# Starting the FFN products of two tiles one projection group later, with the additions of their banks

## The chip, the cores and the metric

One Trainium2 chip, one core of it. The metric is the device time of one launch in microseconds (us), the median of the runs of one kernel. Engines are named as the profile names them: PE is TensorE (matmuls and transposes), DVE is VectorE, ACT is ScalarE, POOL is GpSimd, SP is SyncE, which issues the DMAs.

## The reference

Input `x` is (8, 1024, 512) in f32. Two branches work on the layer-normed input and are added to it:

```python
xn = layernorm(x)                                   # eps 1e-5
# attention branch
xm = xn * time_mix + shift_by_one_token(xn) * (1 - time_mix)
k = exp(min(xm @ Wk.T, 60)); v = xm @ Wv.T; r = xm @ Wr.T
wkv, sum_k = decayed causal sums over tokens of k*v and of k, per channel
attn = (sigmoid(r) * wkv / (sum_k + 1e-16)) @ Wo.T
# FFN branch: layernorm again (eps 1e-3, gamma, beta), a scale from the
# largest absolute value of the whole tensor, clip to +-128, ternary weight
ffn = clip(xn2 * 128 / gamma) @ w_ternary * (gamma * beta / 128)
out = x + attn + ffn
```

The scale `gamma` of the FFN is a maximum over all eight batches, so no FFN product can start before every batch has been seen. This splits the kernel in two halves.

## The kernel before, in words

A tile is 512 tokens of one batch; a batch has two tiles, 0 and 1. The first half (phase "A") does the attention of batches 0 to 3, writes x + attn of them to a scratch tensor, and prepares the FFN input of all eight batches, with its largest absolute value. The second half (phase "B") does the attention of batches 4 to 7, and the FFN products of all eight: one pass b = 4, 5, 6, 7 handles the tiles of batch b ("own0", "own1") and those of batch b - 4 ("other0", "other1"). The other tiles are read back from scratch into the tile `ZB` ("parked") and the FFN product is added there; the own tiles are added into `X[0]` and `X[1]`.

Each engine has its own program, written out in a fixed order, and semaphores join them. A pass consists of 24 groups, g = 0 to 23. Group g projects one of k, v, r (m = g mod 3) for a chunk c = g div 3 of 128 channels: chunks 0 to 3 are tile 0, chunks 4 to 7 tile 1. A group is 12 matmuls of 512 columns into one bank of `KVR`. Beside it each group works on one of 24 slots: slots 0 to 3 are the four chunks of the FFN input of own0, 4 to 7 of other0, 8 to 11 the time mix of tile 1, 12 to 15 FFN own1, 16 to 19 FFN other1, and 20 to 23 the time mix of the next batch's tile 0. In the second half only the mix slots are transposed on PE. An FFN slot is scaled by ACT (L585), clipped by DVE (L836), split into a high part by ACT (L616, `ffn_hi`) and a low part by DVE (L850, `ffn_lo`). DVE and ACT split slot n while they are at group n + 1: DVE's low part of slot 19, for example, stands at group 20, behind the recurrence of chunk 6 (at group 19), `rwkv_lo` of chunk 5, and the mix of slot 20.

On PE an FFN product (`ffn_out`) is 4 chunks x 4 banks x 2 matmuls = 32 matmuls into the four banks of `OUT`; chunk ch needs the low part of its slot (`dve_lo`). Its place is given by the table `FFN_AFTER`. The attention's output product (`attn_out`) is 4 x 4 x 3 = 48 matmuls into the same four banks: tile 0 behind group 12, tile 1 behind group 23. Its chunk 3 needs DVE's `rwkv_lo` of the last chunk, and in its chunk 0 bank q may only be written when DVE has added the previous contents of bank q to its tile (L942, L944, which count `dve_out`):

```python
if j == 0:
    pe.wait_ge(dve_out, first_bank + q + 1)
```

Where DVE makes these additions is given by the table `ADDS_AT`: group, tile, banks. Within a group of the second half DVE's order is: in groups with m = 2, `rwkv_lo` of the chunk before; the mix or clip of this group's slot (for mix slots it comes first); in the last group of a pass that isn't the last pass, `denominator` of chunk 7, which waits for ACT's logarithm of the sums of chunk 7; the low part of the slot before; the additions of `ADDS_AT`; then, for m = 0, `clamp_k` and `denominator`, for m = 1, `rwkv` of the chunk before and the recurrence of this chunk (L893 to L910). The recurrence of chunk 7 stands at group 22, that of chunk 3 at group 12, behind the additions of that group. The last pass has no slots 20 to 23.

On ACT the evacuation of a mix slot (L575, L576) frees the single transpose bank `TB`, and PE transposes slot n only when slot n - 1 has been evacuated. ACT's evacuation of slot n waits for the low part of slot n - 2.

Of the kernel before, what the change touches and what calls it, by code (L numbers as in the profile page):

```python
# [45 lines left out]

STATS_ORDER = ["other0", "own1", "other1", "next0"]

FFN_AFTER = {4: "own0", 8: "other0", 16: "own1", 20: "other1"}
FFN_TILES = ["own0", "other0", "own1", "other1"]  # L50


# [7 lines left out]
def mixed_decay_kernel(nc, x, time_decay, time_first, time_mix, Wk, Wv, Wr, Wo, Wf, ln_gamma, ln_beta, out):  # L60
# [19 lines left out]
    with ExitStack() as ctx:  # L80
# [330 lines left out]
        def _(pe):  # L411
# [4 lines left out]
            def transpose_slot(b, ph, n, src):  # L416

                _, ch = slot_of(ph, n)
                bank = first_banks[n] if ph == "P" else TB[:, :]
                for q in range(Q):  # L420
                    last = nc.tensor.transpose(bank[:, q * P:(q + 1) * P], src[:, q, ch * P:(ch + 1) * P],  # L421
                                               ident[:, :])
                last.then_inc(pe_t, 1)
# [46 lines left out]
            def project(b, ph, g):  # L470

                c, m = divmod(g, 3)
                t, j = divmod(c, CH)
                w = names[m]
                if m:
                    pe.wait_ge(dve_w, (m + 1) * CH)

                pe.wait_ge((act_k, dve_kv, act_r)[m], CREDIT + CHUNKS * b + c)
                for ch in range(CH):
                    if j == 0 and m == 0:  # L480

                        slot0 = first_slot("mix_own1") if t == 1 else -CH
                        pe.wait_ge(dve_lo, RING + slots_before(b, ph, slot0 + ch) + 1)
                    hi = WH[w][:, ch, j * P:(j + 1) * P]
                    lo = WL[w][:, ch, j * P:(j + 1) * P]
                    nc.tensor.matmul(KVR[:, m, :], hi, XH[t][:, ch, :], start=(ch == 0), stop=False)  # L486
                    nc.tensor.matmul(KVR[:, m, :], hi, XL[t][:, ch, :], start=False, stop=False)  # L487
                    last = nc.tensor.matmul(KVR[:, m, :], lo, XH[t][:, ch, :], start=False, stop=(ch == CH - 1))  # L488
                last.then_inc(pe_g, 1)
# [20 lines left out]
            def ffn_out(b, what):  # L510

                first_bank = bank_use(b, "B", what)
                start_slot = first_slot(f"ffn_{what}")
                for ch in range(CH):
                    pe.wait_ge(dve_lo, RING + slots_before(b, "any", start_slot + ch) + 1)
                    for q in range(Q):
                        if ch == 0:
                            pe.wait_ge(dve_out, first_bank + q + 1)
                        nc.tensor.matmul(OUT[:, q, :], AH[:, ch, q * P:(q + 1) * P], WQ[:, ch, :],  # L519
                                         start=(ch == 0), stop=False)  # L520
                        last = nc.tensor.matmul(OUT[:, q, :], AL[:, ch, q * P:(q + 1) * P], WQ[:, ch, :],  # L521
                                                start=False, stop=(ch == CH - 1))
                        if ch == CH - 1:
                            last.then_inc(pe_out, 1)
                    if ch < CH - 1:
                        last.then_inc(pe_ah, 1)

            def batch(b, ph, is_last=False):
                for g in range(GROUPS):
# [6 lines left out]
                    else:  # L536
                        if n is not None:
                            slot(b, ph, n)
                        project(b, ph, g)
                    if ph == "B" and g in FFN_AFTER:  # L540
                        ffn_out(b, FFN_AFTER[g])
                    if g == ATTN0_AFTER:
# [216 lines left out]
        def _(dve):  # L759
# [166 lines left out]
            def add_out(b, ph, what, banks=None):  # L926
# [12 lines left out]
                for q in range(Q) if banks is None else banks:  # L939
# [3 lines left out]
                    else:  # L943
# [4 lines left out]
            STATS_AT = {4: "own1", 16: "next0"}  # L948

            ADDS_AT = {5: [("own0", [0])], 6: [("own0", [1])], 7: [("own0", [2, 3])],  # L950
# [3 lines left out]

            def batch(b, ph, is_last=False, last_a=False):
                last = None
# [208 lines left out]
```

## Time and profile before

| | |
|---|---|
| median of 3 runs | 951.38 us (951.17 to 952.89) |
| the profiled execution | 954.09 us, span on the core 952.3 us |
| PE busy | 903.3 us, 95% of the span |
| DVE busy | 781.4 us, 82% |
| ACT busy | 522.0 us, 55% |
| POOL busy | 191.0 us, 20% |
| mean granted PE clock | 0.989 of full |

How to read it: a busy PE is not a PE at its peak, since matmuls overlap (each is recorded with some 0.39 us, and the next starts some 0.23 us after it). The second half begins about 465 us from the span's start; passes 5, 6 and 7 begin at about 577, 702 and 827 us. Times below are us from the span's start.

### The profile page before, as it was taken

The numbers are of one execution on the slowest core, as the hardware profiler recorded it, in microseconds if no ns is written. First come the engines' busy times: TensorE is split into PE (matmuls) and PEld (weight loads), VectorE is DVE, ScalarE is ACT, GpSimd is POOL, SyncE is SP. The second block draws the span as 40 slices with busy tenths as digits, with TensorE's granted clock in tenths as the row PEclk, the third lists the DMA queues.
The fourth block names the chain that finished last, engine by engine and source line by source line (L and its number), as shares of the span: only waits on it lengthen the run. The fifth ranks groups of instructions, "written<-read, shape, count | busy, mean of one in ns | idle before, by whom it ended". The sixth has DMA issues, their size and how long they took to land.

```text
span 952.3 us, 13343 instructions
## 1 busy us (share of the span) xinstructions
PE 903.3 (95%) x4162; PEld 734.3 (77%) x4162; DVE 781.4 (82%) x1353; ACT 522.0 (55%) x852; POOL 191.0 (20%) x268
## 2 busy tenths in 40 slices
PE   5689999999999999999999999999999999999998
PEld 5468878777877778777878877778778787787886
DVE  5878898989798989888868887788779787787785
ACT  4366665747574756575554654454646445556442
POOL 4341514234243333240000200202002011020000
PEclk9879999999999999999999999999999999999999
DMA  8120504141422314041504315124052150240502
GB/s 321 66 100 13 200 11 166 66 143 66 143 77 103 118 62 159 28 162 42 189 23 155 111 45 188 32 99 143 27 191 69 58 185 22 98 157 12 175 3 88
DMA packets 50758, 97.89 MB, mean 103 GB/s; under 512 B 3100, under 2 KB 3112, under 8 KB 50728
## 3 DMA queue, kind: packets, MB, share of 16 engines
q1 hardware_dynamic: 50728, 97.54, 29.5%
q8 instruction: 13, 0.21, 0.1%
q14 instruction: 17, 0.14, 0.0%
HBM read 55.58 MB, written 41.94 MB: 102 GB/s over the span
## 4 chain that ended last, share of the span: by engine, by line
DVE 38%; PE 27%; issue 14%; ACT 13%; DMA 3%; POOL 2%; DVEq 1%; ACTq 0%; SPq 0%; POOLq 0%
DVE scans L903 9%; PE kvr L486 5%; PE kvr L488 5%; PE kvr L487 5%; DVE bn_stats L778 4%; DVE rwkv_lo L923 4%; DVE k_and_kv L893 3%; DVE k_and_kv L919 3%; PE out_banks L501 2%; DVE evacuated L826 2%; PE transposed L421 2%; PE out_banks L503 2%; PE out_banks L502 2%; DVE k_and_kv L910 2%; DVE xm_lo L850 2%
## 5 line engine op out<-in xcount | busy, mean ns | idle before, releaser
L1059 POOL TENSOR_SCALAR stat_work<-mean_var 128x4 f32<-128x4 f32 x24 | 7.8, 324 | 549.7 <-DVE mean_var L783 500.7
L519 PE MATMUL out_banks<-w_ternary,ffn_hi 128*128 128x512 f32 x256 | 100.7, 393 | 11.0 <-DVE ffn_lo L850 11.0
L501 PE MATMUL out_banks<-wo_hi,rwkv_hi 128*128 128x512 f32 x256 | 102.6, 401 | 2.0 <-DVE rwkv_lo L923 1.7
L486 PE MATMUL kvr<-xm_hi,wv_hi 128*128 128x512 f32 x256 | 104.5, 408 | 0.0
L486 PE MATMUL kvr<-xm_hi,wk_hi 128*128 128x512 f32 x256 | 104.4, 408 | 0.0
L486 PE MATMUL kvr<-xm_hi,wr_hi 128*128 128x512 f32 x256 | 104.2, 407 | 0.0
L503 PE MATMUL out_banks<-wo_hi,rwkv_lo 128*128 128x512 f32 x256 | 101.3, 396 | 0.0
L502 PE MATMUL out_banks<-wo_lo,rwkv_hi 128*128 128x512 f32 x256 | 101.2, 395 | 0.0
L488 PE MATMUL kvr<-xm_hi,wv_lo 128*128 128x512 f32 x256 | 100.9, 394 | 0.0
L488 PE MATMUL kvr<-xm_hi,wk_lo 128*128 128x512 f32 x256 | 100.9, 394 | 0.0
L487 PE MATMUL kvr<-xm_lo,wv_hi 128*128 128x512 f32 x256 | 100.6, 393 | 0.0
L487 PE MATMUL kvr<-xm_lo,wk_hi 128*128 128x512 f32 x256 | 100.4, 392 | 0.0
L488 PE MATMUL kvr<-xm_hi,wr_lo 128*128 128x512 f32 x256 | 100.4, 392 | 0.0
L521 PE MATMUL out_banks<-w_ternary,ffn_lo 128*128 128x512 f32 x256 | 100.1, 391 | 0.0
L487 PE MATMUL kvr<-xm_lo,wr_hi 128*128 128x512 f32 x256 | 99.7, 389 | 0.0
L1079 POOL TENSOR_SCALAR normed<-x,own_stats 128x512 f32<-128x512 f32 x52 | 78.9, 1524 | 67.6 <-PE transposed L421 59.7
L910 DVE SCALAR_TENSOR_TENSOR k_and_kv<-k_and_kv,first,scans 128x1024 f32<-128x1024 f32 x64 | 84.7, 1324 | 1.1
L580 ACT ACTIVATE evacuated<-transposed,beta_in,gamma_in 128x512 f32<-128x512 f32 x64 | 49.3, 770 | 58.6 <-PE transposed L421 58.6
L903 DVE TENSOR_TENSOR_SCAN scans<-decay,state,k_and_kv 128x512 f32<-128x512 f32 x64 | 79.7, 1289 | 0.0
L903 DVE TENSOR_TENSOR_SCAN scans<-decay,k_and_kv 128x512 f32<-128x512 f32 x64 | 75.0, 1214 | 0.0
L575 ACT ACTIVATE evacuated<-transposed,time_mix 128x512 f32<-128x512 f32 x61 | 41.6, 681 | 58.1 <-PE transposed L421 50.4
L670 ACT ACTIVATE gate<-kvr 128x512 f32<-128x512 f32 x64 | 37.8, 590 | 61.3 <-PE kvr L488 60.9
(125 smaller groups left out, 1988.1 us busy)
## 6 DMA issues: line engine op xcount, KB each, us to landing
x<-in_L_attn_x SPq DMA_DIRECT2D x16, 1024.0 KB, 5.6
ffn_input<-evacuated SPq DMA_DIRECT2D x64, 256.0 KB, 2.4
other<-ffn_input SPq DMA_DIRECT2D x64, 256.0 KB, 2.8
other<-in_L_attn_x SPq DMA_DIRECT2D x8, 1024.0 KB, 5.3
attn_scratch<-x SPq DMA_DIRECT2D x8, 1024.0 KB, 4.4
parked<-attn_scratch SPq DMA_DIRECT2D x8, 1024.0 KB, 6.6
out<-parked SPq DMA_DIRECT2D x8, 1024.0 KB, 4.6
out<-x SPq DMA_DIRECT2D x7, 1024.0 KB, 4.8
```

Source lines behind the costliest of these rows:

```text
L486: nc.tensor.matmul(KVR[:, m, :], hi, XH[t][:, ch, :], start=(ch == 0), stop=False)
L487: nc.tensor.matmul(KVR[:, m, :], hi, XL[t][:, ch, :], start=False, stop=False)
L488: last = nc.tensor.matmul(KVR[:, m, :], lo, XH[t][:, ch, :], start=False, stop=(ch == CH - 1))
L501: nc.tensor.matmul(OUT[:, q, :], hi, WH["o"][:, j, :], start=(j == 0), stop=False)
L502: nc.tensor.matmul(OUT[:, q, :], hi, WL["o"][:, j, :], start=False, stop=False)
L503: last = nc.tensor.matmul(OUT[:, q, :], lo, WH["o"][:, j, :], start=False, stop=(j == CH - 1))
L519: nc.tensor.matmul(OUT[:, q, :], AH[:, ch, q * P:(q + 1) * P], WQ[:, ch, :], start=(ch == 0), stop=False)
L521: last = nc.tensor.matmul(OUT[:, q, :], AL[:, ch, q * P:(q + 1) * P], WQ[:, ch, :], start=False, stop=(ch == CH - 1))
L580: nc.scalar.activation(U[:, r, :], bank, ACT.Identity, bias=bet[:, ch:ch + 1], scale=gam[:, ch:ch + 1]).then_inc(act_u, 1)
L903: last = V.tensor_tensor_scan(S[:, i, 1:TILE + 1], dec, kv[:, i, :], 0.0 if t == 0 else state[:, j, i:i + 1], ALU.mult, ALU.add)
L910: V.scalar_tensor_tensor(kv, kv, first[:, j:j + 1], S[:, :, 0:TILE], ALU.mult, ALU.add).then_inc(dve_sum, 1)
L1079: last = G.tensor_scalar(dst[:, q, :], src[:, q, :], stats[:, 2 * ffn, q:q + 1], stats[:, 2 * ffn + 1, q:q + 1], ALU.mult, ALU.add)
```

## The change

In the second half the FFN products of other0 and other1 are issued by PE behind group 9 and 21 instead of behind group 8 and 20, so they fall behind the transposes of slots 9 and 21 and the k projection of chunks 3 and 7. DVE's additions of other0's banks move from groups 9, 10, 11, 12 (one bank each) to 10 (one), 11 (two) and 12 (one); those of other1 from groups 21 and 22 to 22 and 23, two banks each. Nothing is added or taken out, and the first half is unchanged.

```diff
-FFN_AFTER = {4: "own0", 8: "other0", 16: "own1", 20: "other1"}
+FFN_AFTER = {4: "own0", 9: "other0", 16: "own1", 21: "other1"}
...
             ADDS_AT = {5: [("own0", [0])], 6: [("own0", [1])], 7: [("own0", [2, 3])],
-                       9: [("other0", [0])], 10: [("other0", [1])], 11: [("other0", [2])], 12: [("other0", [3])],
+                       10: [("other0", [0])], 11: [("other0", [1, 2])], 12: [("other0", [3])],
                        17: [("own1", [0])], 18: [("own1", [1])], 19: [("own1", [2, 3])],
-                       21: [("other1", [0, 1])], 22: [("other1", [2, 3])]}
+                       22: [("other1", [0, 1])], 23: [("other1", [2, 3])]}
```

## Rows read from the trace of the kernel before

**Rows 1.** PE's waits from 400 to 952 us: total, times, longest.
```profile
PE out_banks L519 <- DVE ffn_lo L850: 11.0, 7, 2.1
```

**Rows 2.** PE's timeline, other0 of pass 5: start, duration, operation, [idle before <- releaser].
```profile
609.47 0.39 PE L519 MATMUL out_banks<-w_ternary,ffn_hi 128*128 128x512 f32 x1
...
616.16 0.50 PE L519 MATMUL out_banks<-w_ternary,ffn_hi 128*128 128x512 f32 x1 [1.09 <-DVE ffn_lo L850]
...
621.33 0.60 PE L421 MATMUL transposed<-ident,normed 128*128 128x128 f32 x4
...
641.99 0.39 PE L486 MATMUL kvr<-xm_hi,wv_hi 128*128 128x512 f32 x1
```

**Rows 3.** DVE's timeline, the same stretch.
```profile
615.42 0.69 DVE L850 TENSOR_TENSOR ffn_lo<-evacuated,ffn_hi 128x512 fp32r<-128x512 f32 x1
...
630.42 0.68 DVE L893 TENSOR_TENSOR k_and_kv<-k_and_kv,kvr 128x512 f32<-128x512 f32 x1
```

**Rows 4.** PE's timeline, other1 and the output product of pass 5.
```profile
671.49 0.39 PE L519 MATMUL out_banks<-w_ternary,ffn_hi 128*128 128x512 f32 x1
...
678.74 0.50 PE L519 MATMUL out_banks<-w_ternary,ffn_hi 128*128 128x512 f32 x1 [1.65 <-DVE ffn_lo L850]
...
680.69 0.60 PE L421 MATMUL transposed<-ident,normed 128*128 128x128 f32 x4
...
683.90 0.60 PE L421 MATMUL transposed<-ident,normed 128*128 128x128 f32 x4
...
690.30 0.39 PE L501 MATMUL out_banks<-wo_hi,rwkv_hi 128*128 128x512 f32 x1
...
702.15 0.39 PE L486 MATMUL kvr<-xm_hi,wk_hi 128*128 128x512 f32 x1
```

**Rows 5.** ACT's timeline, evacuations of slots 20, 21 and 22 of pass 5.
```profile
671.16 0.68 ACT L576 ACTIVATE shifted_part<-transposed,one_minus_mix 128x512 f32<-128x512 f32 x1
...
681.40 0.69 ACT L575 ACTIVATE evacuated<-transposed,time_mix 128x512 f32<-128x512 f32 x1 [6.95 <-PE transposed L421]
...
685.21 0.68 ACT L575 ACTIVATE evacuated<-transposed,time_mix 128x512 f32<-128x512 f32 x1
```

**Rows 6.** DVE's timeline, groups 20 to 23 of pass 5.
```profile
678.00 0.68 DVE L850 TENSOR_TENSOR ffn_lo<-evacuated,ffn_hi 128x512 fp32r<-128x512 f32 x1
...
686.49 0.15 DVE L823 COPY last_token<-shifted_part 128x1 f32<-128x1 f32 x1 [0.18 <-ACT shifted_part L576]
...
687.76 1.40 DVE L944 SCALAR_TENSOR_TENSOR parked<-out_banks,scalars,parked 128x512 f32<-128x512 f32 x2
...
692.84 1.28 DVE L910 SCALAR_TENSOR_TENSOR k_and_kv<-k_and_kv,first,scans 128x1024 f32<-128x1024 f32 x1
...
695.30 0.69 DVE L915 TENSOR_TENSOR gate<-gate,k_and_kv 128x512 f32<-128x512 f32 x1
695.90 1.29 DVE L850 TENSOR_TENSOR xm_lo<-evacuated,xm_hi 128x512 fp32r<-128x512 f32 x2
```

**Rows 7.** Timeline of the last pass, recurrence and output product of its end.
```profile
936.17 0.69 DVE L893 TENSOR_TENSOR k_and_kv<-k_and_kv,kvr 128x512 f32<-128x512 f32 x1
...
937.65 0.39 PE L501 MATMUL out_banks<-wo_hi,rwkv_hi 128*128 128x512 f32 x1
...
940.53 0.69 DVE L923 TENSOR_TENSOR rwkv_lo<-k_and_kv,rwkv_hi 128x512 fp32r<-128x512 f32 x1
```

**Rows 8.** Stretches: length, busy PE, PEld, DVE, ACT, POOL, PE clock, DMA.
```profile
26.87:30.30 3.43, 3.43 (x10) 2.87 (x11) 3.34 (x4) 3.01 (x7) 0.00 (x0) 0.51 0.02 5
...
491.00:494.50 3.50, 3.50 (x12) 2.81 (x11) 0.00 (x0) 1.19 (x3) 0.00 (x0) 0.51 0.00 0
```

**Rows 9.** PE's timeline, three resumptions behind which the clock was low.
```profile
26.87 1.08 PE L421 MATMUL transposed<-ident,normed 128*128 128x128 f32 x4 [3.93 <-POOL normed L1079]
...
52.02 1.09 PE L421 MATMUL transposed<-ident,other 128*128 128x128 f32 x4 [10.58 <-ACT evacuated L580]
...
489.70 0.50 PE L519 MATMUL out_banks<-w_ternary,ffn_hi 128*128 128x512 f32 x1 [1.78 <-DVE ffn_lo L850]
```

## The prediction

> **What bounds the kernel now.** I read the page first, for the busy shares: PE is busy 95% of the span, DVE 82%. With PE that full, a change of order can only matter where it moves PE's idle time, so the next view is PE's waits over the second half. There is one entry of weight: PE waits seven times, 11.0 us in all, for `ffn_lo`, the low part of an FFN slot [rows 1]. PE's timeline says where. All seven stand in the FFN products of the other tiles, in front of the last of the four chunks: other0 in passes 4, 5, 6, 7, other1 in passes 4, 5, 6. In pass 5 they are 1.09 and 1.65 us [rows 2, 4]. The own tiles' products have none, and other1 of the last pass, which has no mix slots behind it, none either. DVE's timeline gives the reason: the low part of slot 7 ends at 615.42 + 0.69 = 616.11 [rows 3], that of slot 19 at 678.68 [rows 6], and PE resumes 0.05 us later each time. DVE works nearly without a gap before, since the recurrence stands in front. So two places of each pass wait for DVE's arrears, and the rest of the pass is PE's own work, but for a few tenths in front of chunk 3 of the output products.
>
> **What a wait costs.** Idle is counted from the modelled end of the last matmul, 0.39 us after its start, while the next would have started 0.23 us after it, and the first matmuls behind a wait are slower by some 0.15 us. So the wait of 1.65 costs 1.65 + 0.16 + 0.15, about 1.95 us, and that of 1.09 about 1.4 us.
>
> **Other0, product behind group 9.** PE's piece from the product's start to the transposes of slot 10 (product, transposes of slot 9, k) takes 621.33 - 609.47 = 11.86 us [rows 2]. With transposes and k in front (3.2 us, as 683.90 - 680.69 [rows 4]) the last chunk is asked for at about 618.1, and its low part is there at 616.1: the wait is gone with 2 us to spare, and the piece is 11.86 - 1.4 = 10.46 us. What is late next is DVE. The output product behind group 12 is paced at its chunk 3 by `rwkv_lo` of chunk 3, which hangs on the recurrence of chunk 3, which starts at 630.42 [rows 3], 9.09 us behind the transposes of slot 10. Between these two points DVE now has one bank's addition more (0.66 us from start to start), bank 0 having moved from group 9 to group 10, and gets some 0.1 back, since `exp_k` of chunk 3 no longer comes late. So of PE's 1.4 us about 0.55 is lost again, and the output product, which ended at 641.99 [rows 2], ends 0.85 us sooner. Passes 6 and 7 are alike. In pass 4 the wait is 1.78 us [rows 9] and behind it the granted clock is 0.51 for 3.5 us [rows 8], which is the lower level (1.2 GHz) and costs half of that, 1.7 us; less 0.6 us for the evacuation of slot 8, which is later there, the gain is 0.85 + 0.7 + 1.6 - 0.6, about 2.5 us. Sum of other0: 3 x 0.85 + 2.5 = **5.1 us gained**.
>
> **Other1, product behind group 21, PE up to the output product.** The transposes of slot 21 now follow group 20 at once, and find slot 20 evacuated at 671.16 + 0.68 = 671.84 [rows 5], 0.4 us behind 671.49 [rows 4]. The product then starts at 675.1 and asks for its last chunk at 680.5, when the low part has been there since 678.68. PE is 1.95 - 0.4 = 1.55 us sooner at the transposes of slot 22 (682.35) and at the output product: 690.30 - 1.55 = 688.75 [rows 4].
>
> **Other1, the additions.** This is the term that decides. The output product writes banks 0 and 1 in its first six matmuls, and at 688.75 + 6 x 0.233 = 690.15 wants bank 2, so DVE must have added bank 2 of other1 by then. Before, that addition stood at group 22, in front of the recurrence of chunk 7: it started at 687.76 [rows 6], in time. Now it stands at group 23. In front of it on DVE lie the whole recurrence of chunk 7, `rwkv_lo` of chunk 6, the mix of slot 23, the early `denominator` of chunk 7 with its wait for ACT's logarithm, and the low part of slot 22. When does DVE get there? ACT starts an evacuation 0.71 us behind the start of its transposes (681.40 against 680.69 [rows 4, 5]) and DVE takes the slot up 1.3 us behind that (686.49 - 685.21 [rows 5, 6]). For slot 22 ACT was held before, by `exp_k` of chunk 7, to 685.21 [rows 5]; this holds no more, as the k projection now precedes the product. So DVE takes up slot 22 at 682.35 + 0.71 + 1.30 = 684.36 instead of 686.49 [rows 6], 2.13 us sooner, and from there to the recurrence it has the same work as before, two additions among it. The last step of the recurrence then starts at 692.84 - 2.13 = 690.71, the denominator at 695.30 - 2.13 = 693.17, the low part of slot 22 at 695.90 - 2.13 = 693.77 [rows 6], the addition of bank 2 at 694.4, and with 0.74 us it ends at 695.1. PE stands from 690.15 to 695.15: **a wait of 5.0 us that was not there**. The addition of bank 3 follows at once and is in time. Behind the wait 42 of 48 matmuls are left, 42 x 0.233 + 0.15 = 9.95 us, so the product ends at 705.1 against 702.15 [rows 4]: 2.95 us later. `rwkv_lo` of chunk 7 costs nothing there: it is ready about 698.4, and chunk 3 of the product comes at 702.2. The next pass starts with PE and carries the delay on in full. Three passes: 3 x 2.95 = **8.85 us lost**.
>
> **Other1 of the last pass.** There was no wait to gain. The output product starts at 937.65 [rows 7] as before and wants bank 2 at 939.05. The recurrence starts when v is projected, some 1.1 us before its 936.17 (two additions no longer stand directly in front of it), runs 940.53 - 936.17 = 4.36 us to `rwkv_lo` of chunk 6 [rows 7], 0.6 us more to the addition, which ends at 940.8: a wait of 1.75 us, **2.0 us lost**. No early denominator stands there in this pass.
>
> **The clock.** The trace of before does not show a wait of 5 us in the second half, so its effect on the granted clock is bounded by neighbours. Below: of the seven waits of 1.1 to 2.1 us [rows 1] one was followed by the low level, the one at 489.70. Above: the two long idle times of the prologue, 3.93 and 10.58 us [rows 9], were both followed by it, the first for 3.4 us at 0.51 [rows 8], the second for the next 5.6 us of matmuls. So a case costs 1.7 us (up to 2.8), and three passes 0 to 8.4 us. A wait of 5.0 us lies nearer to the 3.93, and I take three cases at 1.7 us: **5.1 us lost**; the 42 matmuls behind the wait are then PE's alone and pay it in full.
>
> The Trainium skill (TensorE: Matmul & The Clock Gate, the part on HAM oscillation) tells of a kernel whose bursts of matmuls were separated by waits for a DMA, and which started every burst at the half rate. By that rule all three passes pay; by the share of the seven short waits only 3 x 1.7 / 7 = 0.7 us would be due and the sum would be 6.4 us. Rows of this length in the second half don't exist to tell.
>
> **Transfers.** SP stores the parked tile when the last addition is made, 6 us later than before for other1, and its reload stands in SP's queue behind the store of `X[1]`, which waits for the end of the output product anyway. For other0 the last addition is 0.85 us sooner. I cost both at nothing; the cover is a quarter of a pass, some 30 us.
>
> **Sum.** - 5.1 + 8.85 + 2.0 + 5.1 = + 10.8 us. Against the profiled execution's 954.09 that is 964.9, against the median of the runs 951.38 it is **962.2 us**. (The profiled execution is 2.7 us above the median; nothing in the sum scales with that, save that pass 4's low clock, 1.6 us, may not occur in every run.)
>
> **The rivals.**
> - *The wait comes, the clock holds* in most passes. Then the sum is + 5.7 to + 7.4, 957.1 to 958.8 us. For it speaks that six of seven waits did nothing to the clock; against it that both idle times above 3.9 us did.
> - *The clock stays low for longer*, as behind the 10.58 us: 2.8 us each, + 14.1, 965.5 us.
> - *The other side: DVE is in time.* The additions of banks 2 and 3 would have to end before 690.15. Then other0 gives 5.1 and other1 3 x 1.55 = 4.65: 951.4 - 9.75 = 941.6 us. For it: DVE stands idle 4 us in front of slot 21 before, and its work could slide forward. Against it: what precedes the addition is a chain that starts only when slot 22 is transposed and v of chunk 7 projected, behind the moved product. It decides at about 693.1: if bank 2 is added by then (a wait of 3.0 us) and the clock holds, gain and loss cancel.
> - *Nothing moves*, because DVE's arrears only show up as other waits of the same length: 951 us. For other0 that is nearly so (0.55 of 1.4 lost again); for other1 the chain gives no reason for equality.
>
> **How the numbers follow.** Wait and low clock in two or three passes 0.62; wait with the clock held 0.20; longer low clock 0.10; in time 0.05; nothing 0.03. The likeliest is 962.2. The range takes in the held clock and the longer one, 956.5 to 966.5. A measurement of this kernel can tell about 0.2%, 1.9 us. Only the last two cases, and part of the held clock with a shorter wait, lie below + 1.9: faster 0.04, same 0.03, slower 0.93.
>
> **What would show it.** In the profile after: no wait of `out_banks` L519 for `ffn_lo`; a new wait of `out_banks` L501 for `parked` L944, three of some 5.0 us and one of 1.75; PE's first half unchanged; the clock at 0.5 for some 3.4 us behind each of the three; the recurrence of chunk 3 about 0.85 us sooner relative to group 8. The prediction is wrong if DVE reaches group 23's additions sooner than 693, or if the clock pays nothing.

## The result, and the profile after

| | before | after |
|---|---|---|
| median | 951.39 us | 964.62 us (964.26 to 964.76, 4 runs) |
| ratio to before | | 1.014, 95% interval 1.0128 to 1.0152 |
| the profiled execution | 954.09 us | 964.76 us |
| span of it | 952.3 us | 963.0 us |
| mean granted PE clock | 0.989 | 0.981 |

Slower by 13.2 us; 10.8 were forecast (962.2, range 956.5 to 966.5). The two profiled executions lie only 10.7 us apart, because that of before was itself 2.7 us above its median: it has the low clock in pass 4 [rows 8], and it spent 1.2 us more in the first half, which the change does not touch (pass 4's first projection starts at 449.87 before and at 448.63 after).

PE's waits after, from 400 to 963 us (total, times, longest), answer to [rows 1]:

```profile
PE out_banks L501 <- DVE parked L944: 16.3, 4, 4.9
...
PE out_banks L501 <- DVE rwkv_lo L923: 1.6, 4, 0.4
```

The entry of before, 11.0 us for `ffn_lo`, is gone. In its place stands a wait of the output product for DVE's additions, four times: 4.86, 4.87, 4.86 and 1.68 us, where the forecast said 5.0, 5.0, 5.0 and 1.75.

PE's timeline after, pass 5, which answers to [rows 4]:

```profile
672.23 0.66 PE L421 MATMUL transposed<-ident,normed 128*128 128x128 f32 x4 [0.25 <-ACT shifted_part L576]
...
682.51 0.39 PE L521 MATMUL out_banks<-w_ternary,ffn_lo 128*128 128x512 f32 x1
...
689.15 0.39 PE L501 MATMUL out_banks<-wo_hi,rwkv_hi 128*128 128x512 f32 x1
...
690.31 0.40 PE L503 MATMUL out_banks<-wo_hi,rwkv_lo 128*128 128x512 f32 x1
695.57 0.80 PE L501 MATMUL out_banks<-wo_hi,rwkv_hi 128*128 128x512 f32 x1 [4.87 <-DVE parked L944]
696.16 0.63 PE L502 MATMUL out_banks<-wo_lo,rwkv_hi 128*128 128x512 f32 x1
...
700.43 0.43 PE L503 MATMUL out_banks<-wo_hi,rwkv_lo 128*128 128x512 f32 x1
700.70 0.40 PE L501 MATMUL out_banks<-wo_hi,rwkv_hi 128*128 128x512 f32 x1
...
707.70 0.39 PE L486 MATMUL kvr<-xm_hi,wk_hi 128*128 128x512 f32 x1
```

The 0.25 us in front of the transposes of slot 21 is the wait for the evacuation of slot 20; with the 0.16 us that idle time leaves out it costs the 0.4 of the forecast. The output product starts at 689.15, writes banks 0 and 1 in six matmuls, stands 4.87 us in front of bank 2, and then runs 12 matmuls in 5.13 us (695.57 to 700.70), a mean of 0.43 us from start to start, before it is back at 0.23. From start to end it takes 18.55 us, where it took 11.85 before. The clock says the same (stretches behind the wait: length, busy PE, PEld, DVE, ACT, POOL, PE clock, DMA share, GB/s):

```profile
695.50:700.00 4.50, 4.43 (x10) 3.47 (x11) 2.57 (x5) 1.24 (x2) 0.00 (x0) 0.50 0.62 233
700.00:707.70 7.70, 7.70 (x33) 6.19 (x32) 1.78 (x3) 0.00 (x0) 0.00 (x0) 0.97 0.00 0
```

DVE's timeline after, the same end of pass 5, against [rows 6]:

```profile
684.76 0.15 DVE L823 COPY last_token<-shifted_part 128x1 f32<-128x1 f32 x1 [2.10 <-ACT shifted_part L576]
...
686.03 1.40 DVE L944 SCALAR_TENSOR_TENSOR parked<-out_banks,scalars,parked 128x512 f32<-128x512 f32 x2
...
691.11 1.28 DVE L910 SCALAR_TENSOR_TENSOR k_and_kv<-k_and_kv,first,scans 128x1024 f32<-128x1024 f32 x1
692.31 0.69 DVE L923 TENSOR_TENSOR rwkv_lo<-k_and_kv,rwkv_hi 128x512 fp32r<-128x512 f32 x1
692.91 0.15 DVE L823 COPY last_token<-shifted_part 128x1 f32<-128x1 f32 x1
692.97 0.68 DVE L826 TENSOR_TENSOR evacuated<-evacuated,shifted_part 128x511 f32<-128x511 f32 x1
693.57 0.69 DVE L915 TENSOR_TENSOR gate<-gate,k_and_kv 128x512 f32<-128x512 f32 x1
694.17 0.69 DVE L850 TENSOR_TENSOR xm_lo<-evacuated,xm_hi 128x512 fp32r<-128x512 f32 x1
694.77 1.40 DVE L944 SCALAR_TENSOR_TENSOR parked<-out_banks,scalars,parked 128x512 f32<-128x512 f32 x2
```

The additions of banks 0 and 1 stand in front of the recurrence, those of banks 2 and 3 behind the recurrence and behind `rwkv_lo` of chunk 6, the mix of slot 23, the denominator of chunk 7 and the low part of slot 22. Bank 2 is added by 694.77 + 0.74 = 695.5, and PE resumes at 695.57. Note also the 2.10 us in front of 684.76. DVE stands idle from 682.66, and the last matmul of the FFN product starts at 682.51: the banks have just been finished, and DVE waits for ACT to evacuate slot 22 instead of emptying them.

### The profile page after: what moved, and what is told of

It reads as the page before. It is cut to its first block, busy times and chain, and to the rows that moved or that the text cites. A ratio compares the mean times of both kernels' runs of the same rounds, so it can differ in the third digit from the quotient of the medians.

```text
span 963.0 us, 13339 instructions
## 1 busy us (share of the span) xinstructions
PE 907.5 (94%) x4162; PEld 736.7 (76%) x4162; DVE 780.4 (81%) x1353; ACT 522.0 (54%) x852; POOL 191.1 (20%) x268
## 4 chain that ended last, share of the span: by engine, by line
PE 40%; DVE 31%; ACT 11%; issue 11%; DMA 2%; POOL 2%; DVEq 0%; ACTq 0%; SPq 0%; POOLq 0%
DVE scans L903 7%; PE kvr L488 7%; PE kvr L486 7%; PE kvr L487 7%; PE out_banks L521 4%; PE out_banks L519 4%; DVE bn_stats L778 4%; PE out_banks L501 3%; PE out_banks L502 3%; PE out_banks L503 3%; DVE rwkv_lo L923 3%; PE transposed L421 2%; DVE k_and_kv L893 2%; DVE k_and_kv L919 2%; DVE k_and_kv L910 2%
## 5 line engine op out<-in xcount | busy, mean ns | idle before, releaser
L501 PE MATMUL out_banks<-wo_hi,rwkv_hi 128*128 128x512 f32 x256 | 105.5, 412 | 18.5 <-DVE parked L944 16.3
L502 PE MATMUL out_banks<-wo_lo,rwkv_hi 128*128 128x512 f32 x256 | 103.7, 405 | 0.0
L503 PE MATMUL out_banks<-wo_hi,rwkv_lo 128*128 128x512 f32 x256 | 103.6, 405 | 0.0
L501 PEld LDWEIGHTS out_banks<-wo_hi,rwkv_hi 128*128 128x128 f32 x256 | 49.8, 195 | 35.0 <-DVE parked L944 18.0
```

Source lines behind the costliest of these rows:

```text
L501: nc.tensor.matmul(OUT[:, q, :], hi, WH["o"][:, j, :], start=(j == 0), stop=False)
L502: nc.tensor.matmul(OUT[:, q, :], hi, WL["o"][:, j, :], start=False, stop=False)
L503: last = nc.tensor.matmul(OUT[:, q, :], lo, WH["o"][:, j, :], start=False, stop=(j == CH - 1))
```

## The experiments

Eight kernels, each timed beside the kernel before on the same chip. The kernel before gave 950.72 us beside the first four and 951.09 us, on another chip, beside the last four; the ratios below are to these. The changed kernel was not timed again there, so a difference to its 964.62 us is uncertain by some tenths of a us more.

**One half of the change alone.** First other0 alone:

```diff
-FFN_AFTER = {4: "own0", 9: "other0", 16: "own1", 21: "other1"}
+FFN_AFTER = {4: "own0", 9: "other0", 16: "own1", 20: "other1"}
...
-                       22: [("other1", [0, 1])], 23: [("other1", [2, 3])]}
+                       21: [("other1", [0, 1])], 22: [("other1", [2, 3])]}
```

> Only the other0 half of the change: its product behind group 9, its additions at groups 10, 11, 12; other1 as before the change. My theory: the wait for the low part of slot 7 goes in all four passes, and 0.55 of its 1.4 us comes back through the recurrence of chunk 3, so 4 x 0.85 = 3.4 us less than before the change: 948.0 us. Rival 1 (the whole wait is gained): 4 x 1.4 = 5.6 less, 945.8. Rival 2 (other0 takes part in the loss): 951.4 or more.

Measured 947.97 us, ratio 0.9969 (0.9958 to 0.9981). Other0's half is a gain, and of the size of the first theory; 945.8 lies outside the interval (0.9958 x 950.72 = 946.7). PE's waits of the second half in it:

```profile
PE out_banks L519 <- DVE ffn_lo L850: 4.9, 3, 1.7
PE out_banks L501 <- DVE rwkv_lo L923: 2.8, 7, 0.4
```

Only other1's three waits for a low part are left. Of the seven for `rwkv_lo` three stand in tile 1, as before the change (1.1 us in all), and four, of 0.42 us each, are new in tile 0: tile 0's output product takes 11.9 us in place of 11.5, and this is where a part of other0's gain went.

Then other1 alone, the same two edits the other way round (8 for other0, with its additions at groups 9 to 12):

> Only the other1 half of the change: its product behind group 21, its additions at groups 22 and 23; other0 as before the change. My theory: all of the loss sits here, three passes of about 5.1 us (the profile after shows 4.8, 5.2 and 5.4) and 1.9 in the last, 17.3 us over before the change: 968.7 us. Rival (the two halves don't simply add, since the delays share DVE's arrears): clearly less than 968, say 965.

Measured 968.7 us, ratio 1.0175 (1.0155 to 1.0195). The rival's 965 lies just under the lower end of the interval (1.0155 x 950.72 = 965.5). That the halves add is compatible with the numbers, and no more: - 2.75 and + 17.98 make + 15.2 by the medians, and the interval of other1 alone, + 14.7 to + 18.5, leaves room for the 13.2 measured together. The profiles agree better, as the part on the prediction shows.

**The place of two additions.** The product stays behind group 21, and only DVE's table is edited:

```diff
-                       22: [("other1", [0, 1])], 23: [("other1", [2, 3])]}
+                       22: [("other1", [0, 1, 2, 3])]}
```

> The changed kernel with all four additions of other1 at group 22, so in front of the recurrence of chunk 7; PE's order stays as changed. My theory (the place of two additions behind the recurrence is the whole cause): no wait for bank 2 and no low clock; four additions in front of the recurrence leave rwkv_lo of chunk 7 some 0.8 us sooner than before the change and the output product waits about 1.2 us for it, so 3 x 0.8 and 4 x 0.85 less than before the change: 945.6 us. Rival (the later place of the product on PE is the cause): it stays near 964.6.

Measured 944.87 us, ratio 0.9936 (0.9924 to 0.9948). Two additions moved by one group turn a loss of 13 us into a gain of 6, and the rival is out. No wait for `parked` is left; from 500 us on PE's entry for the output product is

```profile
PE out_banks L501 <- DVE rwkv_lo L923: 5.0, 7, 1.1
```

which is 0.41 us in each tile 0 and, in three passes, the 1.11 us that four additions in front of the recurrence cost at chunk 3 of tile 1.

**The additions in DVE's gap.** The changed kernel with a second table, worked off at the end of a group:

```diff
-                       10: [("other0", [0])], 11: [("other0", [1, 2])], 12: [("other0", [3])],
+                       10: [("other0", [2])], 11: [("other0", [3])],
...
-                       22: [("other1", [0, 1])], 23: [("other1", [2, 3])]}
+                       22: [("other1", [3])]}
+            LATE_ADDS = {9: [("other0", [0, 1])], 21: [("other1", [0, 1, 2])]}
...
+                    for what, banks in (LATE_ADDS.get(g, ()) if ph == "B" else ()):
+                        add_out(b, ph, what, banks)
```

> The changed kernel with the additions put where DVE stands idle while PE works on the product: other0's banks 0 and 1 at the end of group 9, 2 at group 10, 3 at group 11; other1's banks 0, 1, 2 at the end of group 21 and 3 at group 22. DVE's gap in front of slot 22 is 2.1 us in the profile after, three additions take 2.0. My theory: all waits of PE in these stretches go, 1.65 us per pass for other0 and 2.1 us in each of three passes for other1, 12.9 less than before the change: 938.5 us. Rival (the additions wait for the product's banks in the gap and push the mix slots back): nearer to 945.

Measured 937.85 us, ratio 0.9857 (0.9843 to 0.9871): 1.4% faster than the kernel before and the fastest of all. DVE's timeline of its pass 5:

```profile
676.14 2.06 DVE L944 SCALAR_TENSOR_TENSOR parked<-out_banks,scalars,parked 128x512 f32<-128x512 f32 x3
678.31 0.15 DVE L823 COPY last_token<-shifted_part 128x1 f32<-128x1 f32 x1
```

Three additions fill the gap and the mix of slot 22 follows without idle time. The output product then runs through: it starts at 682.70 and the next k projection at 693.89, 11.19 us. All seven that are followed by a projection take this long, where the kernel with four additions at group 22 had four of 11.9 us and three of 12.6: that is 6.9 of the 7.0 us between the two.

**The additions in the gap, products where they were.** The same idea on the kernel before, all four additions at the end of groups 8 and 20:

```diff
-                       9: [("other0", [0])], 10: [("other0", [1])], 11: [("other0", [2])], 12: [("other0", [3])],
...
-                       21: [("other1", [0, 1])], 22: [("other1", [2, 3])]}
+            LATE_ADDS = {8: [("other0", [0, 1, 2, 3])], 20: [("other1", [0, 1, 2, 3])]}
```

> The kernel before, products behind groups 8 and 20 as they were, with the additions alone moved into DVE's gap: all four of other0 at the end of group 8 and all four of other1 at the end of group 20. The waits of PE for the low parts of slots 7 and 19 stay. The small waits in front of chunk 3 of the output products go, 0.34 us for tile 0 in four passes and 0.66 for tile 1 in three: 3.3 us less than before the change, 947.5 on this chip's 950.7. Rival (the additions alone give what the kernel with both moves gave): 938.

Measured 947.44 us, ratio 0.996 (0.9946 to 0.9973). Its waits for low parts stay:

```profile
PE out_banks L519 <- DVE ffn_lo L850: 9.9, 7, 1.8
```

Its output products take 11.2 us too, so the rival (938) is out and the additions alone give 3.6 us. The later place of the products is worth another 9.2 us (each against the kernel before beside it; 9.6 by the plain medians), but only with the additions in time.

**The additions first in group 23.** They still stand behind the recurrence, but in front of all the rest:

```diff
-                       22: [("other1", [0, 1])], 23: [("other1", [2, 3])]}
+                       22: [("other1", [0, 1])]}
...
+                    if ph == "B" and g == GROUPS - 1:
+                        add_out(b, ph, "other1", [2, 3])
                     if m == 2 and c and c != CH and g != ATTN0_AFTER - 1:
                         rwkv_lo(b, c - 1)
```

> The changed kernel, with the additions of other1's banks 2 and 3 as DVE's first work of group 23, directly behind the recurrence of chunk 7, instead of behind rwkv_lo, the mix of slot 23, the early denominator and a low part. The addition starts 2.46 us sooner (692.31 instead of 694.77 in the profile after), so the wait is 2.4 us long instead of 4.86. My theory: 3 x 2.46 and 0.6 in the last pass less than the changed kernel if the low clock still comes, 956.6 us; and 6.3 less again if it doesn't, 950.3. By the seven waits of 1.1 to 2.1 us before the change, one of which was followed by it, it should come in few of the three: I take 951.5. Rival (the early denominator's wait for ACT, not DVE's order, sets the addition): no more than 1 us less than the changed kernel.

Measured 954.11 us, ratio 1.0028 (1.0016 to 1.0039). The wait is as long as expected, in each of three passes, but in the profiled execution the low clock came in all three (PE's timeline and the stretch behind the wait, pass 4):

```profile
564.63 0.80 PE L501 MATMUL out_banks<-wo_hi,rwkv_hi 128*128 128x512 f32 x1 [2.41 <-DVE parked L944]
565.22 0.63 PE L502 MATMUL out_banks<-wo_lo,rwkv_hi 128*128 128x512 f32 x1
```

```profile
564.60:568.00 3.40, 3.37 (x8) 2.70 (x9) 3.40 (x7) 1.30 (x3) 0.00 (x0) 0.52 0.54 205
```

The product takes 15.33, 15.41 and 15.42 us, where 11.2 + 2.41 + 0.3 = 13.9 would do: 1.4 to 1.5 us each for the clock. (This is one execution; the timed ones lie between 951.77 and 956.19.) The theory of the order held; my 951.5, which took the clock to hold in most passes, missed by 2.6 us, and lies outside the interval (952.6 to 954.8). The value for the low clock in all passes, 956.6, lies outside too. It counted 2.1 us for each, and a fall costs 1.45 us here, which is 2 of the 2.5 us between. The rival about the denominator falls, since the kernel is 10.5 us faster than the changed one.

**PE kept busy in the wait.** Extra matmuls in front of the wait, whose results nobody reads. They write the k bank, and the added wait on `act_k` makes sure that ACT has read it:

```diff
+                        if ph == "B" and t == 1 and j == 0 and q == 2 and not (isinstance(b, int) and b == LAST_PASS):
+                            pe.wait_ge(act_k, CREDIT + CHUNKS * b + CHUNKS)
+                            for _ in range(FILL):
+                                nc.tensor.matmul(KVR[:, 0, :], RH[:, 0, 0:P], WH["o"][:, 0, :], start=True, stop=True)
                         if j == 0:
                             pe.wait_ge(dve_out, first_bank + q + 1)
```

With `FILL` = 20:

> The changed kernel, with 20 more matmuls of 512 columns on PE in front of the wait for bank 2 in passes 4, 5 and 6; they write the k bank, which is free there, and their result is never read. They take some 4.6 of the 5.0 us in which PE would stand idle. My theory (the wait costs its own length, and the low clock behind it costs some 2.1 us more, because PE was idle): DVE's addition comes when it came, the clock holds, and the output product takes 16.4 us instead of 18.2 to 18.7: 3 x 2.1 less than the changed kernel, 958.3 us. Rival (the low clock has another cause than PE's idle time, or the slow matmuls are paid for anyway): no less than 964, or more by what the extra matmuls take.

Measured 958.06 us, ratio 1.0072 (1.0054 to 1.009): 6.5 us less than the changed kernel, with 60 matmuls more, though still slower than the kernel before. PE's timeline and the stretch behind the wait, pass 5:

```profile
689.07 4.83 PE L503 MATMUL kvr<-wo_hi,rwkv_hi 128*128 128x512 f32 x20
694.14 0.50 PE L507 MATMUL out_banks<-wo_hi,rwkv_hi 128*128 128x512 f32 x1 [0.24 <-DVE parked L950]
```

```profile
694.10:700.00 5.90, 5.86 (x25) 4.74 (x26) 2.53 (x4) 1.25 (x2) 0.00 (x0) 1.00 0.48 178
```

The product still resumes when DVE has added bank 2, and the clock stays at full; the output products take 16.33, 16.37 and 16.37 us in place of 18.18, 18.55 and 18.73. The loss is thus two things, the wait and the clock behind it, and this run parts them. It also clears the transfers: behind the wait 178 GB/s for 5.9 us are as many bytes as the 233 GB/s for 4.5 us of the changed kernel, at the full clock.

With `FILL` = 10, so that about half of the wait stays idle:

> As the kernel with 20 extra matmuls whose results are never read, but with 10, so that PE works for 2.3 us and then stands idle for some 2.7 us. The output product's dates are the same. If the length of PE's idle stretch decides on the clock, as the waits of 1.1 to 2.1 us suggest, most passes hold it: 958.5 to 960.5 us. If the clock falls at any wait above 2.5 us, 964.5.

Measured 961.15 us, ratio 1.0103 (1.0083 to 1.0124), between the two values named, a little above the first (interval 959.0 to 962.9, which leaves 964.5 out). The profiled execution shows how: the same wait of 2.54 us twice, passes 5 and 6, with a different end:

```profile
697.21 0.50 PE L507 MATMUL out_banks<-wo_hi,rwkv_hi 128*128 128x512 f32 x1 [2.54 <-DVE parked L950]
...
825.84 0.50 PE L507 MATMUL out_banks<-wo_hi,rwkv_hi 128*128 128x512 f32 x1 [2.54 <-DVE parked L950]
```

```profile
697.20:702.00 4.80, 4.79 (x14) 3.80 (x15) 2.51 (x4) 1.24 (x2) 0.00 (x0) 0.66 0.58 218
825.80:830.00 4.20, 4.17 (x18) 3.36 (x19) 2.53 (x4) 1.25 (x2) 0.00 (x0) 1.00 0.63 237
```

Pass 4, with 2.57 us, had the low clock too: two of three, so the clock did not hold in most passes, as the first value assumed. The two falls cost 1.6 us each (output products of 17.93 and 17.87 us against 16.32).

## Why the prediction was right, step by step

- **Other0, 5.1 us gained.** The profiled executions give 2.40 us in pass 4 (67.20 to 64.80 from the first projection to the end of tile 0's output product), 0.84 (64.74 to 63.90), 0.80 and 1.31 in passes 5, 6 and 7: 5.35, against 2.5 + 3 x 0.85. The product behind group 9 waits no more, and 0.41 us now stand in front of chunk 3 of the output product, as the step on DVE's extra addition said. Two things in it were misread. Passes 6 and 7 are not alike: pass 7's wait before is 2.08 us (the longest in [rows 1]), and it gained 1.31. And 1.6 us of the sum was the low clock of pass 4, which is not a part of the median that it was subtracted from: in the profiles of other1 alone and of the additions in the gap with the products in their old place, the same wait of 1.77 us is not followed by it. The prediction named this doubt and still counted the term. By the medians other0 alone gained 2.75 us (1.8 to 4.0), 2.35 less than the 5.1 forecast.
- **Other1, PE sooner at the output product by 1.55 us.** In pass 5, from the end of tile 0's output product to the start of tile 1's: 690.30 - 641.99 = 48.31 before, 689.15 - 642.32 = 46.83 after, 1.48 us.
- **Other1, the additions.** The wait was worked out as 5.0 us from the last matmul's due end and is 4.87 by the profile's count, 5.03 by starts (695.57 - 690.31 - 0.23). Behind 684.76 every row of DVE came in the order and at the distance that the working named; the whole stretch, PE's part too, lies 0.40 us later than the times named. That these two additions' place is the whole cause is shown by the kernel with all four at group 22: it has PE's new order, and is faster than before. From the end of tile 0's output product to the next pass this half lost 4.81, 5.22 and 5.36 us, where 2.95 + 1.7 = 4.65 was forecast; nearly all of the difference is the clock's.
- **The last pass, 2.0 us.** The wait is 1.68 us, and the pass's second part took 1.9 us longer. The parts, - 5.35 + 15.39 + 1.90 and the - 1.24 of the first half, give the 10.7 us between the two profiled executions.
- **The clock, 3 x 1.7 us.** It fell in all three passes, as assumed, and its share is shown by the kernel with the filled wait. The size was short: it was to be low for some 3.4 us, and in pass 5 it was for 5.1. The 42 matmuls behind the wait took 11.76, 12.13 and 12.31 us instead of the 9.95 of the forecast (9.90 in the kernel with the filled wait), 2.1 us each by the mean. The filled wait gave 6.5 / 3 = 2.2. That makes the forecast 1.3 to 1.5 us too low, and other0's term makes it 1.6 us too low or somewhat more; together this is a little above the 2.4 us that it was short. That the clock would fall at all was a choice between neighbours on both sides, not something worked out; it came true, but the miss at 2.41 us shows that where it changes was not known.
- **Transfers, nothing.** The parked tile of pass 5 is stored at 696.20 instead of 689.20, 7.0 us later, and PE has no wait for a transfer in the second half after the change.
- **The rivals.** The clock that holds is out for a wait of 4.9 us. The clock that stays low for longer, 2.8 us each, gave 965.5, which is nearer to the 964.62 than the forecast; but the 2.1 us measured is nearer to 1.7 than to 2.8, and the rival is near because its surplus makes up for other0's term. The side on which DVE is in time did not happen. It had 941.6; the two kernels that bring DVE in time run in 944.87, with four additions in front of the recurrence, and 937.85, with them in the gap, one 3.3 us above and one 3.7 below. That nothing moves is out.

What stays open is why one of two waits of 2.54 us is followed by the low clock and the other is not. No run here shows it.

## What to carry to other kernels

A consumer that writes a buffer again waits for the engine that empties it, so when a product is moved, look where the emptying stands in the other engine's fixed order: it must lie in front of the long chain (here a recurrence of some 4.4 us); one step later was already behind it. When an engine stands idle just behind the end of a product, as DVE did here for 2.1 us, that gap is the place for the work that empties the product. And a long wait on PE inside a dense stream can cost more than its length, by the half-rate matmuls behind it: here 1.4 to 2.5 us more behind 11 of the 12 waits of 2.4 us and above.

## What the runs showed of the hardware that was not expected

Waits of PE of 0.9 us and more in the second half, over the profiled executions of all ten kernels, one of each, and how many were followed by the low level (0.5 of full, 1.2 GHz):

| length of the wait | cases | followed by the low level |
|---|---|---|
| 0.97 to 1.78 us | 30 | 1 |
| 2.08 and 2.09 us | 2 | 1 |
| 2.41 to 2.57 us | 6 | 5 |
| 4.86 and 4.87 us | 6 | 6 |

I had placed 2.4 us with the short ones; in these executions it belongs with the long ones. What a fall costs varied with the length too: 1.4 to 1.6 us behind 2.41 to 2.57 us and 1.8 to 2.5 us behind 4.87 us, where up to 13 matmuls ran at 0.43 us. And extra work without any use, put into the wait, made the changed kernel 6.5 us faster.
